# Projection of an attention layer: halves of heads as row tiles, values copied by ScalarE, their bias added after the attention

## The reference, cut to what matters

```python
def rope(Y):                      # theta, cos and sin are tables
    Y2 = jnp.concatenate([-Y[..., d // 2:], Y[..., :d // 2]], axis=-1)
    return Y * cos + Y2 * sin
q = split_heads(x @ Wq.T + bq); k = split_heads(x @ Wk.T + bk); v = split_heads(x @ Wv.T + bv)
q, k = rope(q), rope(k)
att = softmax(where(tril, q @ k.T / sqrt(16), -inf))
x = layernorm(x + (att @ v) @ Wo.T + bo)
h = gelu(tlin(gelu(tlin(silu(tlin(x, w1)) * tlin(x, w2), h1)), h2))   # tlin: product, then a scale per column
out = layernorm(x + tlin(h, w3))
```

## Time and profile before

| | |
|---|---|
| time, median of 3 runs | 2792.42 us (2791.34 to 2792.55) |
| the profiled execution's own time | 2795.36 us |
| its span | 2793.6 us |
| mean granted TensorE clock in it | 0.989 |
| busy share of the span: PE, DVE, ACT, POOL | 98%, 68%, 48%, 5% |
| last instruction of the projection on VectorE | ends 133.4 us after the start |

### The profile page before, as it was taken

One profiled execution on the slowest core, in us unless ns is written; L12 is line 12 of the kernel. 1 busy time (PEld: TensorE's weight loads), 2 busy tenths in 40 slices (PEclk: granted clock), 3 DMA queues, 4 the chain that ended last, 5 costly groups with the idle time before them and its releaser, 6 DMA issues.

```text
span 2793.6 us, 39368 instructions
## 1 busy us (share of the span) xinstructions
PE 2729.1 (98%) x14880; PEld 1424.9 (51%) x14880; DVE 1899.9 (68%) x4003; ACT 1348.4 (48%) x2641; POOL 138.3 (5%) x206
## 2 busy tenths in 40 slices
PE   8899999999999999999999999999999999999998
PEld 4423333333333333333323333588888887888887
DVE  6999999888888888888887774633333352443343
ACT  4436666777776777777777776411111111000100
POOL 3300110001100001100000000000000000000000
PEclk9979999999999999999999999999999999999999
DMA  7731110001110011110001000411111132121100
GB/s 217 204 74 39 30 30 26 3 15 32 29 43 6 5 33 32 30 34 3 1 3 39 19 5 9 118 58 58 58 58 58 43 128 108 46 82 54 45 16 23
DMA packets 95613, 133.47 MB, mean 48 GB/s; under 512 B 31462, under 2 KB 69094, under 8 KB 91718
## 3 DMA queue, kind: packets, MB, share of 16 engines
q1 hardware_dynamic: 81452, 96.25, 10.7%
q0 software_dynamic: 6336, 23.34, 3.8%
q10 hardware_dynamic: 7648, 11.54, 1.5%
HBM read 83.77 MB, written 47.32 MB: 47 GB/s over the span
## 4 chain that ended last, share of the span: by engine, by line
PE 88%; DVE 6%; issue 2%; ACT 1%; DMA 1%; SPq 0%; ACTq 0%; POOLq 0%; POOL 0%; DVEq 0%
PE wi_f L984 19%; PE at_o L533 18%; PE at_row L498 17%; PE at_key L512 16%; PE na_h L1202 13%; PE na_y L1214 3%; DVE at_segmax L584 3%; DVE fr_masked L580 1%; DMA values<-pr_vals 1%; ACT at_probs L648 1%; PE at_key L515 1%; PE wi_p L833 1%; DVE pr_parts L252 0%; DVE pr_full L248 0%; PE pr_main L130 0%
## 5 line engine op out<-in xcount | busy, mean ns | idle before, releaser
L648 ACT ACTIVATE at_probs<-at_key 128x512 f32<-128x512 f32 (+3 forms) x2304 | 1127.3, 567 | 502.4 <-PE at_key L512 353.2
L584 DVE TENSOR_REDUCE at_segmax<-at_row 128x1 f32<-128x512 f32 x1792 | 1142.8, 684 | 169.2 <-PE at_row L498 164.9
L512 PE MATMUL at_key<-fr_q_stack,fr_k_stack 99*128 99x512 bf16 (+3 forms) x1152 | 415.0, 365 | 1.3 <-ACT at_probs L648 1.0
L498 PE MATMUL at_row<-fr_k_stack,fr_q_stack 96*128 96x512 bf16 (+3 forms) x1152 | 404.6, 376 | 10.8 <-DVE at_mask L612 5.5
L498 PE MATMUL at_row<-at_k_stack,at_q_stack 96*128 96x512 bf16 (+3 forms) x1152 | 408.1, 364 | 1.8 <-DVE at_segmax L584 1.1
L512 PE MATMUL at_key<-at_q_stack,at_k_stack 99*128 99x512 bf16 (+3 forms) x1152 | 402.2, 364 | 7.5 <-ACT at_probs L648 6.9
L1202 PE MATMUL na_h<-fr_h,fr_h2w_h 128*128 128x512 f32 x1024 | 322.1, 396 | 1.4 <-DVE fr_h L730 1.4
L533 PE MATMUL at_o<-at_probs,fr_values 128*32 128x512 f32 (+3 forms) x2304 | 289.0, 574 | 0.0
L533 PE MATMUL at_o<-at_probs,at_values 128*32 128x512 f32 (+3 forms) x2304 | 287.9, 572 | 0.0
L580 DVE CUSTOM_DVE_ANT_0 fr_masked<-at_row,fr_causal 128x384 f32<-128x384 f32 (+3 forms) x512 | 243.8, 483 | 45.1 <-PE at_row L498 44.7
L498 PEld LDWEIGHTS at_row<-fr_k_stack,fr_q_stack 96*128 96x128 bf16 x1152 | 110.3, 99 | 308.3 <-DVE at_segmax L584 160.1
(11 more groups left out here) (121 smaller groups left out, 2558.1 us busy)
## 6 DMA issues: line engine op xcount, KB each, us to landing
hidden<-wi_h SPq DMA_DIRECT2D x64, 256.0 KB, 2.0
na_h2f<-hidden SPq DMA_DIRECT2D x8, 1024.0 KB, 7.7
q_parts<-pr_parts SPq DMA_DIRECT2D x48, 128.0 KB, 2.4
k_parts<-pr_parts SPq DMA_DIRECT2D x48, 128.0 KB, 3.3
at_q_stack<-q_parts POOLq DMA_DIRECT2D x48, 128.0 KB, 3.5
at_k_stack<-k_parts POOLq DMA_DIRECT2D x48, 128.0 KB, 3.8
values<-pr_vals SPq DMA_DIRECT2D x32, 136.0 KB, 3.3
outputs<-at_outs SPq DMA_DIRECT2D x128, 34.0 KB
```

Source lines behind the costliest of these rows:

```text
L498: last = nc.tensor.matmul(bank[:, 0:w], qst[u][0:SROWS, c, h, i * P:(i + 1) * P], kst[u][0:SROWS, h, s * CH:s * CH + w], start=True, stop= ...
L512: last = nc.tensor.matmul(bank[:, q0:CH], kst[u][0:SROWS + PARTS, h, j * P:(j + 1) * P], qst[u][0:SROWS + PARTS, c, h, q0:CH], start=True, ...
L584: nc.vector.tensor_reduce(segmax[:, n % 2, h * TPC + i, s:s + 1], row_ps[r % RING_R][:, 0:w], op=ALU.max, axis=AX.X).then_inc(rows_taken, 1)
L648: nc.scalar.activation(probs[:, g % RING_P, h, q0:CH], key_ps[m % RING_K][:, q0:CH], ACT.Exp).then_inc(probs_ready, 1)
```

## The change

The rows of Wq and Wk (and their biases) are laid out by half: row tile 0 holds the first 8 dimensions of all 16 heads, row tile 1 the other 8. A rotated partner then sits on the same partition of the other tile. The matmul with `turn` and its PSUM banks go. A pair g of tiles (q or k of a chunk, 16 pairs in all) is the new unit: TensorE computes both halves and then always the values of 256 tokens; ScalarE copies both halves; VectorE multiplies both by the sines in one instruction of 1024 elements a partition, reading `pr_lin` in SBUF; it subtracts for one half and adds for the other. The casts and differences are done for 1024 elements at a time. Parts of a half are stored in one DMA (two for a pair), to interleaved rows, and `parts` has 3 slots of pairs.

The values are copied to SBUF by ScalarE (`take_values`), in one instruction, without the bias. The bias is added to the normalised attention output by two further VectorE instructions in `Prepare.scale`. `load_first` moves from ScalarE's queue to SyncE's. In `attend` TensorE waits later for the casts and for the last values.

```diff
-    UNITS = 2 * DH
-    NU = UNITS * NCH
+    PAIRS = 2
+    NU = PAIRS * NCH
     BUFS = 3
-    SLOTS = 4
+    SLOTS = 3
...
             def main(g):
...
-            def rotate(g):
...
-                nc.tensor.matmul(rot_ps[g % 2][:, :], turn[:, :], lin[:, g % 3, :], start=True, stop=True).then_inc(rot_ready, 1)
+                for half in range(2):
+                    if g >= 2:
+                        pe.wait_ge(lin_ready, 2 * (g - 2) + half + 1)
+                    bank = main_ps[2 * (g % 2) + half]
...
-            main(0)
             for g in range(NU):
-                if g + 1 < NU:
-                    main(g + 1)
-                rotate(g)
-                if g % 2 == 1:
-                    values(g // UNITS, g % UNITS // 2)
+                main(g)
+                values(*divmod(g, PAIRS))
...
             def linear(g):
...
-                nc.scalar.activation(lin[:, g % 3, :], main_ps[g % 3][:, :], ACT.Identity, bias=bias[:, m:m + 1],
...
+                for half in range(2):
+                    act.wait_ge(main_ready, 2 * g + half + 1)
+                    if g >= 2:
+                        act.wait_ge(t1_ready, 2 * (g - 2) + half + 1)
+                        act.wait_ge(t2_ready, g - 1)
+                    nc.scalar.activation(lin[:, g % 2, half, :], main_ps[2 * (g % 2) + half][:, :], ACT.Identity,
+                                         bias=bias[:, 2 * m + half:2 * m + half + 1],
...
+            def take_values(n, i):
...
+                    act.wait_ge(v_stored[i], 32 * n)
+                act.wait_ge(v_ready, 2 * n + i + 1)
+                nc.scalar.activation(vals[:, i, :, :, 0:HD], v_ps[i][:, :, :].rearrange("p j (h d) -> p j h d", d=HD), ACT.Copy
+                                     ).then_inc(v_taken, 1)
...
             for g in range(NU + 1):
                 if g + 1 < NU:
                     linear(g + 1)
                 if g < NU:
-                    act.wait_ge(full_ready, g + 1)
+                    take_values(*divmod(g, PAIRS))
+                    act.wait_ge(full_ready, 2 * g + 2)
                     if g >= SLOTS:
-                        act.wait_ge(parts_stored[g % SLOTS], 16 * PARTS * (g // SLOTS))
-                    nc.scalar.activation(parts[:, g % SLOTS, 0, :], full[:, g % 2, :], ACT.Copy).then_inc(hi_ready, 1)
+                        act.wait_ge(parts_stored[g % SLOTS], 16 * 2 * (g // SLOTS))
+                    nc.scalar.activation(parts[:, g % SLOTS, 0, :, :], full[:, g % 2, :, :], ACT.Copy).then_inc(hi_ready, 1)
...
-                if 2 <= n < 2 + FIRST_EARLY:
...
-                    front.load_first(act, qp_d, kp_d, n - 2, range(m, len(TERMS), UNITS))
...
         @block.gpsimd
...
+                for half in range(2):
+                    pool.wait_ge(lin_ready, 2 * g + half + 1)
+                    if g >= 2:
+                        pool.wait_ge(full_ready, 2 * (g - 2) + half + 1)
+                    nc.gpsimd.tensor_tensor(t1[:, g % 2, half, :], lin[:, g % 2, half, :], cos[:, n % BUFS, :], ALU.mult
+                                            ).then_inc(t1_ready, 1)
...
             for g in range(NU + 2):
...
-                    dve.wait_ge(rot_ready, g + 1)
-                    nc.vector.tensor_tensor(t2[:, g % 2, :], rot_ps[g % 2][:, :], sin[:, n % BUFS, :], ALU.mult
+                    dve.wait_ge(lin_ready, 2 * g + 2)
+                    if g >= 1:
+                        dve.wait_ge(full_ready, 2 * g)
+                    nc.vector.tensor_tensor(t2[:, :, :], lin[:, g % 2, :, :],
+                                            sin[:, n % BUFS, :].unsqueeze(1).broadcast_to([P, 2, CH]), ALU.mult
                                             ).then_inc(t2_ready, 1)
...
-                    nc.vector.tensor_tensor(full[:, g % 2, :], t1[:, g % 2, :], t2[:, g % 2, :], ALU.add
-                                            ).then_inc(full_ready, 1)
+                    for half, op in enumerate((ALU.subtract, ALU.add)):
+                        dve.wait_ge(t1_ready, 2 * g + half + 1)
+                        nc.vector.tensor_tensor(full[:, g % 2, half, :], t1[:, g % 2, half, :], t2[:, 1 - half, :], op
+                                                ).then_inc(full_ready, 1)
...
-                if g < NU and m % 2 == 1:
...
-                    if n > 0:
-                        dve.wait_ge(v_stored[i], 32 * n)
-                    for j in range(2):
-                        last = nc.vector.tensor_tensor(
-                            vals[:, i, j, :, 0:HD], v_ps[i][:, j, :].rearrange("p (h d) -> p h d", d=HD),
-                            bv[:, :].rearrange("p (h d) -> p h d", d=HD), ALU.add)
-                    last.then_inc(v_taken, 1)
...
             for g in range(NU):
+                if 0 <= early < FIRST_EARLY:
...
+                    front.load_first(sp, qp_d, kp_d, early, range(m, len(TERMS), PAIRS))
                 sp.wait_ge(parts_ready, g + 1)
+                for half in range(2):
+                    sp.dma_start((qp_d, kp_d)[m].rearrange("a (p f) n t -> f p a n t", f=2)[half, :, :, n, :],
+                                 parts[:, g % SLOTS, :, half, :]).then_inc(parts_stored[g % SLOTS], 16)
+                sp.wait_ge(v_taken, g + 1)
+                for j in range(2):
+                    sp.dma_start(v_d[:, :, n, 2 * m + j, :].rearrange("q p e -> p q e"),
+                                 vals[:, m, j, :, :].rearrange("p (q h) e -> p q (h e)", q=NQUAD)
+                                 ).then_inc(v_stored[m], 16)
...
+                    if n == 0:
+                        pe.wait_ge(consts_ready, 2)
...
-            pe.wait_ge(consts_ready, 2)
-            for name in ("lin_ready", "t2_ready", "v_taken"):
-                pe.wait_ge(*projected[name])
+            pe.wait_ge(*projected["lin_ready"])
...
                     done = before[QUAD * g + h]
+                    if (n, j, h) == (0, 0, 0):
+                        pe.wait_ge(*projected["v_taken"])
...
         for a in range(DH):
             self.nc.vector.tensor_tensor(o[:, n % 2, a, :], o[:, n % 2, a, :], self.front.recip[:, :], ALU.mult
+                                         ).then_inc(self.scaled, 1)
+        for a in range(DH):
+            dve.wait_ge(self.scaled, DH * n + a + 1)
+            self.nc.vector.tensor_scalar(o[:, n % 2, a, :], o[:, n % 2, a, :], self.front.bv[:, a:a + 1], None, ALU.add
                                          ).then_inc(self.y_ready, 1)
 
...
```

More of the change, by code:

```diff
@@ L72, in project @@
         w = [sb(f"w{a}", [P, DH, D]) for a in "qkv"]
-        turn = sb("turn", [P, P])
-        bias = sb("bias", [P, UNITS])
-        bv = sb("bv", [P, D])
+        bias = sb("bias", [P, 2 * PAIRS])
         xt = sb("xt", [P, BUFS, DH, CH])
@@ L78, in project @@
         sin = sb("sin", [P, BUFS, CH])
-        lin = sb("lin", [P, 3, CH])
-        t1 = sb("t1", [P, 2, CH])
+        lin = sb("lin", [P, 2, 2, CH])
+        t1 = sb("t1", [P, 2, 2, CH])
         t2 = sb("t2", [P, 2, CH])
-        full = sb("full", [P, 2, CH])
-        rest = sb("rest", [P, 2, CH])
-        parts = sb("parts", [P, SLOTS, PARTS, CH], BF16)
+        full = sb("full", [P, 2, 2, CH])
+        rest = sb("rest", [P, 2, 2, CH])
+        parts = sb("parts", [P, SLOTS, PARTS, 2, CH], BF16)
         vals = sb("vals", [P, 2, 2, HEADS, VW])
-        main_ps = [ctx.enter_context(nc.psum_tensor(f"pr_main{i}", [P, CH], F32)) for i in range(3)]
-        rot_ps = [ctx.enter_context(nc.psum_tensor(f"pr_rot{i}", [P, CH], F32)) for i in range(2)]
+        main_ps = [ctx.enter_context(nc.psum_tensor(f"pr_main{i}", [P, CH], F32)) for i in range(4)]
         v_ps = [ctx.enter_context(nc.psum_tensor(f"pr_v{i}", [P, 2, D], F32)) for i in range(2)]
         w_loaded = [sem(f"w{a}_loaded") for a in "qkv"]
-        turn_loaded = sem("turn_loaded")
         bias_loaded = sem("bias_loaded")
-        bv_loaded = sem("bv_loaded")
         bias_ready = sem("bias_ready")
@@ L115, in load_weight, with load @@
             queue.dma_start(w[i][:, :, :], io[name].rearrange("(c p) o -> p c o", p=P)).then_inc(w_loaded[i], 16)
+        def load(queue, n):
+            u = n % BUFS
+            queue.dma_start(xt[:, u, :, :], io["xT"][n]).then_inc(x_loaded[u], 16)
+            queue.dma_start(cos[:, u, :], io["cos"][n]).then_inc(cos_loaded[u], 16)
+            queue.dma_start(sin[:, u, :], io["sin"][n]).then_inc(sin_loaded[u], 16)
         @block.tensor
@@ L119, in main @@
             def main(g):
[L121 removed]
+                n, m = divmod(g, PAIRS)
                 if m == 0:
                     pe.wait_ge(x_loaded[n % BUFS], 16 * (n // BUFS + 1))
[L124 to L141 removed]
+                if n == 0:
+                    pe.wait_ge(w_loaded[m], 16)
+                for half in range(2):
+                    if g >= 2:
+                        pe.wait_ge(lin_ready, 2 * (g - 2) + half + 1)
+                    bank = main_ps[2 * (g % 2) + half]
+                    for c in range(DH):
```

(16 more changed lines are left out.)

103 lines of the change are left out of this document (29 added, 74 removed).

## The result

| | before | after |
|---|---|---|
| time, median | 2791.88 us (2790.97 to 2792.55, 4 runs) | 2870.96 us (2869.79 to 2872.74, 4 runs) |
| span of the profiled execution | 2793.6 us | 2869.7 us |
| mean granted TensorE clock | 0.989 | 0.974 |
| the projection's last instruction on VectorE ends | 133.4 us | 213.3 us |

The ratio is 1.0284, with a 95% interval of 1.0266 to 1.0302: slower, by 79 us. The forecast was 2855, with a range of 2822 to 2878.

A forecast was written before the change was run, and what follows sets the result against it. TensorE, busy 98% of the span, was taken to bound the kernel outside the projection. The projection's end moves from 133.4 to 196 us, +63: 2795.4 + 63 = 2858, less 2.9 to the median, 2855; range 2822 to 2878.

The forecast's parts named there:

- The closed loop: Projection: values copy waits for the store of two pairs earlier, with hi queued behind it; 10.8 us a pair without lock.
- X to H: From the end of VectorE's turn (X) to the end of hi on ScalarE (H): stores, landing, copy, hi, semaphores, 7.2 us.
- H to X: From the end of hi to VectorE's next turn end: rest 1.14, two sums 1.20, last part 1.23, 3.6 us.
- the lock in 8 of 13 loops: GpSimd products block VectorE instructions with both inputs in SBUF, 2 x 1.08 us; 8 loops of 12.9, 5 of 10.8.
- The start: Projection's first turns, 0 to 2, before the loops: VectorE done with them at 28 us.
- The sum: Projection's end on VectorE: 28 + 157 + 11 = 196 us, where it was 133.4; +63 us.
- Costs taken as nothing: Bias instructions, early loads on SyncE and TensorE's work in the projection: covered, zero; uncovered, 1.5 us (first chunk's bias), 3 (loads).
- rival 3: TensorE's clock stays low in projection and first attention rows, and landings take 5.4 us: 2876 to 2887 us; chance 0.09.
- Behind the projection: All that follows the projection is shifted as it is, with no further gain or cost.
- The signs: Trace after: ScalarE waits 3 to 5 us 14 times, part stores 10 to 13 us apart, projection ends at 180 to 200.
- rival 1: The loop without the lock, 9.7 us a pair in the projection: +31, 2823 us; chance 0.22.
- No loop: Rival 2: values stored before ScalarE reaches the copy, VectorE and GpSimd set the pace, 6.8 us a pair: 2785 us; chance 0.06.

The follow-up runs named there:

- store_first: The changed kernel, but SyncE issues the store of a pair's values ahead of the store of its parts: 2803.3 us, ratio 1.0044 to before.
- no_bias_copy_last: The changed kernel with ScalarE copying the values last in its turn (2801.7 us) and the two values' bias instructions a chunk left out: 2803.2 us, 1.0039 to before.
- small_products: The changed kernel, but GpSimd multiplies only 16 of 512 columns by the cosines: 2842.5 us, ratio 1.0181 to before.
- four_buffers: The changed kernel with four buffers of values in place of two, orders unchanged: 2789.1 us, ratio 0.9988 to before.
- psum_only: The changed kernel, but the multiplication by the sines (t2) reads PSUM in two instructions, q's scale folded into its weights: 2871.7 us, ratio 1.0286 to before.
- vector_values: The changed kernel, but VectorE copies the values as the last instruction of its turn, two buffers kept: 2864.8 us, ratio 1.0259 to before.

## Why the prediction was right, step by step

- *The closed loop.* Right. It is the chain of after, and each of three single edits that open it (an order on ScalarE, an order on SyncE, two more buffers) takes 68 to 82 us off, where the change had added 79.
- *X to H, 7.2 us.* 7.6 measured: the stores 1.67 for 1.5, the landing 4.34 for 3.9, the copy 0.5 for 0.62, `hi` 1.06 for 1.05. Over all stores of values after 100 us the landing has a median of 4.1 and never falls under 3.6, where it was 3.0. I had put the growth down to the 768 KB of parts issued just ahead. No run shows that or excludes it: in store_first the median from 110 to 145 us is 4.1 as well, but there too each store goes out right behind a pair of part stores (110.46 and 111.40). In every run the values follow parts or loads, so what makes these stores slower than before stays open.
- *H to X, 3.6 us, and the lock in 8 of 13 loops.* This is the mis-sized step, by 5 x 2.16 = 11 us. VectorE and the lock measured 5.7 in every loop but the last. I had thought that three input loads, some 1.5 us of issue, would stand ahead of `mid` and `linear` on ScalarE and let the products fall into the wait. In after they do not:

```profile
104.78 0.60 ACT L172 ACTIVATE pr_vals<-pr_v 128x512 f32<-128x512 f32 x1 [9.93 <-DMA values<-pr_vals]
104.98 0.34 ACTq L113 DMA_DIRECT2D pr_xt<-in_xT  x1
105.27 1.05 ACT L191 ACTIVATE pr_parts<-pr_full 128x1024 bf16<-128x1024 f32 x1
105.34 0.46 ACTq L114 DMA_DIRECT2D pr_cos<-in_cos  x1
105.83 0.45 ACTq L115 DMA_DIRECT2D pr_sin<-in_sin  x1
106.22 1.05 ACT L194 ACTIVATE pr_parts<-pr_rest 128x1024 bf16<-128x1024 f32 x1
107.17 1.25 ACT L161 ACTIVATE pr_lin<-pr_main,pr_bias 128x512 f32<-128x512 f32 x2
```

  In the text the loads stand behind `mid`. They went out from 104.98 on, beside the copy, `hi` and `mid`, whose activations run without a gap, and `linear` starts 2.4 us after the copy, as in a turn without loads (118.09 and 120.48). The trace of before had it already. There the three input loads, with early loads behind them, go out from 46.14 on beside `hi` and `mid` (46.51 and 47.03), which stand ahead of them in the text; the `linear` behind them starts when the last of seven issues is out, at 50.86:

```profile
46.14 0.36 ACTq L167 DMA_DIRECT2D pr_xt<-in_xT  x1
...
50.98 0.69 ACT L178 ACTIVATE pr_lin<-pr_main,pr_bias 128x512 f32<-128x512 f32 x1 [3.33 <-issue]
```

- *The start.* 31.3 for 28. Turn 0 went as priced. Turn 1 took 5.7 for 4.6 and turn 2 7.7 for 5.8, since more products fell beside VectorE than the one that I had put there: `rest` took 2.00 and `full` 2.36 in turn 1, t2 2.08 and `full` 3.42 in turn 2.
- *The sum.* 31.3 + 13 x 13.14 + 11.1 = 213.3, the measured end, for 28 + 157 + 11 = 196. Of the 17 us the start has 3.3 and the tail 0.5. The loops have 13.6: the lock 10.8, landing 5.7, issue 2.2, less 1.6 for the copy, 1.7 for the semaphores (0.13 a loop in the forecast, and no piece of their own in the chain) and 2.1 for the one short step of 11.0 (191.15 to 202.16), in which no pair is left to multiply: `full` takes 1.28 there and the last part 1.22. These add up to 13.3.
- *Costs taken as nothing.* The bias: no_bias_copy_last. `load_first` on SyncE: its six issues from 114.91 to 117.8 lie within the landing. What they move may still cost: the six steps with such loads (70.77 to 152.14) have a mean of 13.56 us, the other six full ones 13.08, so some 3 us in all; no run leaves these loads out. TensorE has a granted clock of 0.63 to 0.84 in the loop, where it was at 1.00, and waits 64.3 us for the copy, but behind the first 17 us it is on no piece of the chain. So the low clock of rival 3 came in part and cost nothing in the loop. Its second term was no change at all: the first rows of the attention run at 0.50, the lower level, in after (213 to 240 us) and did so before (133 to 160). Its landings of 5.4 did not come.
- *Behind the projection.* Forecast: shifted as it is. Right by the medians: they lie 79.1 us apart, and the projection ends 79.9 us later. The two profiled spans lie only 76.1 apart. The first exponentials start at 238.87 for 158.17 (80.7), the first silu at 1855.0 for 1778.9 (76.1), so some 4 us go between these. But the profiled execution of before, 2795.4, was itself 3.5 above its median, and that of after 0.5, which is enough to make such a difference; nothing shows that the change gives time back there.
- *The signs.* VectorE's wait for `hi` and the wait on the DMA of values, 14 times, came. Four other points missed: ScalarE waits 9.6 us each time (133.9 / 14), not 3 to 5; part stores are 12.9 to 13.9 us apart, not 10 to 13; the projection ends at 213.3, not 180 to 200; VectorE's busy time does not fall (107.4 for 106.6), only its share. The first follows from the forecast's own pieces: ScalarE is done with `linear` 2.2 us after H, X comes at 5.7, and 5.4 of stores and landing follow, which makes 8.9.
- *How near it was.* The time lies 16 us above the forecast and 7 below the top of the range, which had been built with landings of 5.4 that did not come. The mechanism carried the forecast; that the range held is in part owed to that wide end.
- *Rivals.* Without the lock: what small_products made of it, 2842, is above rival 1's 2823; landing and stores are longer than its low ends. No loop: excluded in this kernel; with the loop opened, four_buffers came to 2789 where that rival said 2785.

## What to carry to other kernels

Before a copy is moved to a less busy engine, ask what is queued behind it there, and how far its buffer's last store lies ahead of it, counted in turns of the engine that sets the pace. Before, the store of a buffer left two turns after its copy and the buffer was wanted after four. The change doubled a turn and halved that distance: the store still leaves two turns after the copy, and the buffer is wanted after two. That was too near, whichever engine copied; four turns were enough in both kernels (4 us above before and 3 below it), and three were not tried. A circle of waits multiplies its pieces by the number of turns, so the cheapest cut (a place in a queue, or another buffer) comes first. Work on one piece first can be worth nothing (psum_only) or give only that piece (small_products), and what was hidden shows up afterwards (DMA engines full for 40 us here). The sign of such a circle is a stretch in which every engine is idle for much of each turn and one wait comes once a turn; look at windows shorter than a turn too, since the mean hid DMA engines that were at 0.92 during the landing.

## What the runs showed of the hardware

- DMA issues written in ScalarE's stream went out beside its activations: three, 104.98 to 106.28, while the copy, `hi` and `mid` ran without a gap. An activation written behind them waited only for what outlasted those ahead: nothing in after, but 3.33 us in before, behind seven issues. That is part of the 13.7 us of issue in the earlier trace rows.
- A store of 128 rows of 4 x 68 values landed in 3.0 us before (median from 100 us on) and in 4.1 after, each time behind stores of parts, and in 6.5 to 9.3 with input loads issued 2 us before it (vector_values, five turns).
- A product of GpSimd that fell wholly beside VectorE's instructions with both inputs in SBUF cost them 1.05 to 1.1 us: 2.36 + 2.22 against 1.31 + 1.17 with two small products, and 1.08 in the earlier trace rows. It loses time itself too: 1.5 us in after, 1.26 where VectorE stands (vector_values).
